# A cross-attention stack, second layer: the output bias as one product of three bf16 parts, reciprocals a quarter ahead, queries ahead at the layer's borders

## The reference, cut to what matters

```python
# L1: 32 query heads of 8, 8 key/value heads
q, k, v = x @ Wq + bq, ctx @ Wk + bk, ctx @ Wv + bv
attn = softmax(q k^T / sqrt(8) + mask)          # over 64 context tokens
out  = (attn v).reshape(b, l, H) @ Wo + bo
x    = layer_norm(out + x) * gamma + beta
```

## Time and profile before

| what | us |
|---|---|
| runs | 1150.19, 1145.28, 1144.76 |
| median | 1145.28 |
| the profiled execution | 1143.87 |
| its span, first to last instruction | 1141.9 |
| PE busy | 1062.1 (93% of the span) |
| DVE, ACT, POOL busy | 626.7, 490.8, 400.0 |
| mean granted clock of TensorE | 0.98 |

### The profile page before, as it was taken

The page is one execution under the profiler, slowest core; times in us unless marked ns, Lnnn a source line. Parts: engine busy times, 40 slices in busy tenths (PEclk is TensorE's granted clock), DMA queues, the critical chain, the costliest instruction groups (busy, mean ns, idle before and its releaser), DMA issues.

```text
span 1141.9 us, 17046 instructions
## 1 busy us (share of the span) xinstructions
PE 1062.1 (93%) x6804; PEld 814.2 (71%) x6804; DVE 626.7 (55%) x1070; ACT 490.8 (43%) x988; POOL 400.0 (35%) x415
## 2 busy tenths in 40 slices
PE   6999899999799799998999999999999999978998
PEld 3666455555567588877777777777777777657997
DVE  3656787787566522761455445675444544564552
ACT  2556676676566322214333233333233333324543
POOL 2534477778866411310221222232122211222230
PEclk9999998998999899999999999999999999999999
DMA  9000000000000350000000013310000000100000
GB/s 309 30 2 1 1 1 1 1 1 1 1 2 1 113 201 1 1 1 1 1 1 1 1 38 111 111 38 1 1 1 1 1 1 6 70 0 1 28 20 28
DMA packets 17043, 32.22 MB, mean 28 GB/s; under 512 B 3522, under 2 KB 8388, under 8 KB 16452
## 3 DMA queue, kind: packets, MB, share of 16 engines
q1 hardware_dynamic: 16964, 31.13, 8.0%
HBM read 29.03 MB, written 2.10 MB: 27 GB/s over the span
## 4 chain that ended last, share of the span: by engine, by line
PE 73%; ACT 11%; POOL 7%; DVE 4%; issue 4%; DMA 0%; POOLq 0%; DVEq 0%; ACTq 0%
PE work L740 10%; PE work L852 10%; PE scores L791 9%; PE work L808 5%; PE scores L704 5%; PE work L717 5%; PE work L841 4%; PE work L542 2%; PE work L418 2%; PE work L591 2%; PE scores L533 2%; PE work L823 2%; PE work L499 2%; POOL pair L1747 2%; PE work L894 1%
## 5 line engine op out<-in xcount | busy, mean ns | idle before, releaser
L852 PE MATMUL work<-pair,probsT 128*128 128x256 f32 x512 | 122.1, 393 | 11.0 <-ACT pair L1626 8.8
L740 PE MATMUL work<-ctxT,w 128*128 128x128 f32 x1024 | 120.2, 275 | 3.5 <-ACT pair L1617 1.6
L1706 POOL TENSOR_SCALAR stat<-stat 128x2 f32<-128x2 f32 (+1 forms) x49 | 11.2, 228 | 320.0 <-DVE stat L961 319.0
L852 PEld LDWEIGHTS work<-pair,probsT 128*128 128x128 f32 x512 | 96.9, 194 | 35.9 <-issue 20.3
L740 PEld LDWEIGHTS work<-ctxT,w 128*128 128x128 f32 x1024 | 118.2, 192 | 5.2 <-issue 3.1
L791 PE MATMUL scores<-pair,act_bufs 128*128 128x512 f32 x256 | 115.2, 592 | 0.0
L1617 ACT ACTIVATE pair<-work 128x512 f32<-128x512 f32 x64 | 38.3, 598 | 154.3 <-PE work L808 154.3
L1607 ACT ACTIVATE kvT<-work,cols 128x128 f32<-128x128 f32 x128 | 36.6, 369 | 154.5 <-PE work L740 154.5
L1847 POOL TENSOR_TENSOR probs<-probs,smax 128x1024 f32<-128x1024 f32 x22 | 42.0, 1909 | 159.2 <-DVE smax L1283 159.2
L1263 DVE TENSOR_REDUCE smax<-scores 128x16 f32<-128x1024 f32 x32 | 39.2, 1225 | 77.1 <-PE scores L791 77.1
L791 PEld LDWEIGHTS scores<-pair,act_bufs 128*128 128x128 f32 x256 | 46.3, 190 | 46.0 <-issue 45.9
(11 more groups left out here) (168 smaller groups left out, 2370.9 us busy)
## 6 DMA issues: line engine op xcount, KB each, us to landing
w<-in_l_wk SPq DMA_DIRECT2D x8, 512.0 KB, 6.2
w<-in_l_wq SPq DMA_DIRECT2D x8, 512.0 KB, 7.6
w<-in_l_wv SPq DMA_DIRECT2D x8, 512.0 KB, 7.4
w<-in_l_wo SPq DMA_DIRECT2D x8, 512.0 KB, 8.1
out<-x SPq DMA_DIRECT2D x8, 256.0 KB, 2.2
x<-in_x SPq DMA_DIRECT2D x1, 1536.0 KB, 9.4
pair<-in_l_fc SPq DMA_DIRECT2D x1, 1024.0 KB, 7.1
pair<-in_l_pr SPq DMA_DIRECT2D x1, 1024.0 KB, 9.1
```

The source lines that it names most:

```text
L740: last = mm(bank[:, h * P:(h + 1) * P], w[:, c, (4 * g + h) * K3:(4 * g + h + 1) * K3], ctxT[:, c, p * P:(p + 1) * P], start=(c == 0), sto ...
L852: last = mm(step_banks(j + 1)[0][:, 0:D], probsT_bufs[j % 2][:, q, :], pv[n % 2][:, bb, q, :], start=(q == 0), stop=(q == GH // 2 - 1))
```

## The change

1. **Bias.** The row `l1_bo` is split once, at the end of DVE's slot 5, into three bf16 rows that sum to it, on partitions 0, 32 and 64 of an otherwise zero tile (`bias_parted`, nine operations on 1x256). In `output` one bf16 product of 96 rows of ones with that tile, repeated for both halves, takes the place of two float32 products of one row.
2. **Reciprocals.** In L1's slots ACT spreads them before the second exponential instead of after `probs_out(tiles[0])`; PE transposes them before the fourth scores instead of after `probs_transposed(tiles[1])`; ACT copies them out before `ln_finish`, `key_diagonal` and the third exponential instead of last; DVE normalises before the fourth maximum instead of after it.
3. **Border slot.** PE projects the queries of unit 17 right behind the source of unit 18, ACT copies them out there, and DVE takes the second tile's maximum before the last late sums. Two waits that guard the bank `work[3]` follow this order.
4. **Queries elsewhere.** In L0 and L2 ACT copies the queries out before `key_diagonal` and the layer norm's `ln_finish` instead of last. PE's order there is unchanged.

```diff
+        bias_parts = nc.alloc_sbuf_tensor_at("bias_parts", [P, D], BF16, offset=at + 4 * CTX)
+        bias_rest = nc.alloc_sbuf_tensor_at("bias_rest", [P, D], F32, offset=at + 4 * CTX + 2 * D)
...
             def output(u):
                 if layer == 1:
-                    e.wait_ge(d_bo, 1)
-                    e.wait_ge(p_const, 5)
+                    e.wait_ge(d_part, 9)
+                    e.wait_ge(p_const, 6)
+                    mm(work[2][:, :], ones_bf[0:96, :], bias_parts[0:96, :].unsqueeze(1).broadcast_to([96, TT, D]),
+                       start=True, stop=False, skip_group_check=True)
                 for t in range(TT):
-                    if layer == 1:
-                        mm(work[2][:, t * D:(t + 1) * D], ones[0:1, :], row("l1_bo")[0:1, :], start=True, stop=False)
...
                     probs_transposed(tiles[0])
                     weighted(u - 1)
+                    reciprocals_transposed(u - 1)
                     scores(*tiles_of(u)[3])
                     probs_transposed(tiles[1])
-                    reciprocals_transposed(u - 1)
...
                     source(u + 2)
+                    queries(u + 1)
                     weighted(u - 1)
...
-                if u + 1 < NU:
+                if u + 1 < NU and len(late) < 2:
                     queries(u + 1)
...
+            def bias_parted():
+                bias, part, rest = row("l1_bo"), bias_parts, bias_rest
+                first, second, third = slice(0, 1), slice(32, 33), slice(64, 65)
+                e.wait_ge(d_bo, 1)
+                e.wait_ge(p_const, 6)
+                for r in (first, second, third):
+                    v.tensor_copy(part[r, :], bias[r, :]).then_inc(d_part, 1)
...
                     tile_sums(tiles[0][0])
+                    unit_normal(u - 1)
                     tile_max(*tiles[3])
-                    unit_normal(u - 1)
...
                     unit_queries(u + 1)
+                    reciprocals_spread(u - 1)
                     exponentials(tiles[1])
                     probs_out(tiles[0])
-                    reciprocals_spread(u - 1)
+                    reciprocals_out(u - 1)
                     if ended[0] == 1:
                         ln_finish(("l1", ended[1]), xb(ended[1]), xb(ended[1]))
                     if UNITS[u + 2][0] == 1:
                         key_diagonal(u + 2)
                     exponentials(tiles[2])
                     probs_out(tiles[1])
-                    reciprocals_out(u - 1)
...
                     probs_out(late[1])
                     unit_source(u + 2)
+                    unit_queries(u + 1)
...
                     exponentials(tiles[1])
+                if u + 1 < NU and len(late) < 2:
+                    unit_queries(u + 1)
                 if u + 2 < NU and UNITS[u + 2][0] == 1:
                     key_diagonal(u + 2)
                 if coming[0] == 2:
...
                     ln_finish(("l2", b), xb(b), norm[b % 3])
-                if u + 1 < NU:
-                    unit_queries(u + 1)
```

More of the change, by code:

```diff
@@ L267, in build @@
         d_sum, d_den, d_lrec, d_lr = (sem(f"d_{n}") for n in ("sum", "den", "lrec", "lr"))
-        d_wl, d_sl, d_hl = (sem(f"d_{n}") for n in ("wl", "sl", "hl"))
+        d_wl, d_sl, d_hl, d_part = (sem(f"d_{n}") for n in ("wl", "sl", "hl", "part"))
         p_const, p_rstd, p_kd, p_half, p_sum, p_spr = (sem(f"p_{n}") for n in ("const", "rstd", "kd", "half", "sum", "spr"))
@@ L492, in queries @@
                 e.wait_ge(a_vd, u + 1)
-                if u < 1 or UNITS[u - 1][0] != 1:
+                if u < 2 or 1 not in (UNITS[u - 1][0], UNITS[u - 2][0]):
                     e.wait_ge(a_rT, u - 1)
@@ L551, in reciprocals_transposed @@
                 e.wait_ge(a_qT, min(u + 2, NU))
-                if u + 1 < NU and UNITS[u + 1][0] == 1:
+                if u + 1 < NU and 1 in (UNITS[u][0], UNITS[u + 1][0]):
                     e.wait_ge(a_qT, u + 3)
@@ L584, in output @@
                 if layer == 1:
-                    e.wait_ge(d_bo, 1)
-                    e.wait_ge(p_const, 5)
+                    e.wait_ge(d_part, 9)
+                    e.wait_ge(p_const, 6)
+                    mm(work[2][:, :], ones_bf[0:96, :], bias_parts[0:96, :].unsqueeze(1).broadcast_to([96, TT, D]),
+                       start=True, stop=False, skip_group_check=True)
                 for t in range(TT):
-                    if layer == 1:
-                        mm(work[2][:, t * D:(t + 1) * D], ones[0:1, :], row("l1_bo")[0:1, :], start=True, stop=False)
                     for c in range(DC):
                         last = mm(work[2][:, t * D:(t + 1) * D], oT_bufs[u % 2][:, c, t * P:(t + 1) * P], w[:, c, :],
-                                  start=(layer != 1 and c == 0), stop=(c == DC - 1))
+                                  start=(layer != 1 and c == 0), stop=(c == DC - 1), skip_group_check=True)
                 last.then_inc(pe_wo, 1)
@@ L1076, in output_bias @@
                 v.tensor_tensor(row(f"l{layer}_bo"), work[2][:, 0:D], row(f"l{layer}_bo"), ALU.add).then_inc(d_bo, 1)
+            def bias_parted():
[5 more added lines that the diff above has]
+                    v.tensor_copy(part[r, :], bias[r, :]).then_inc(d_part, 1)
+                e.wait_ge(d_part, 3)
+                for r in (second, third):
+                    v.tensor_tensor(rest[r, :], bias[r, :], part[r, :], ALU.subtract).then_inc(d_part, 1)
+                e.wait_ge(d_part, 5)
+                for r in (second, third):
+                    v.tensor_copy(part[r, :], rest[r, :]).then_inc(d_part, 1)
+                e.wait_ge(d_part, 7)
+                v.tensor_tensor(rest[third, :], rest[third, :], part[third, :], ALU.subtract).then_inc(d_part, 1)
+                e.wait_ge(d_part, 8)
+                v.tensor_copy(part[third, :], rest[third, :]).then_inc(d_part, 1)
             for a in "12":
@@ L1124, in vector @@
                     output_bias(coming[0])
-                for k in late:
-                    tile_sums(k)
+                if late:
+                    tile_sums(late[0])
+                if len(late) == 2:
+                    tile_max(*tiles[1])
+                    tile_sums(late[1])
                 if 0 < u <= NU:
@@ L1131, in vector @@
                     tile_shifted(*tiles[0])
+                if len(late) == 2:
+                    tile_shifted(*tiles[1])
                 if coming[0] == 2:
@@ L1135, in vector @@
                     ln_stats(("l2", b), xb(b), TT)
-                if tiles:
+                if tiles and len(late) < 2:
                     tile_max(*tiles[1])
@@ L1142, in vector @@
                     tile_sums(tiles[0][0])
+                if u == 5:
+                    bias_parted()
             def mlp_norm(b):
@@ L1778, in gpsimd @@
                 g.memset(mask_row[name][:, :], 0.0).then_inc(p_const, 1)
+            g.memset(bias_parts[:, :], 0.0).then_inc(p_const, 1)
             e.wait_ge(p_const, 5)
```

## The result

| kernel | median us | runs | ratio to before, 95% interval |
|---|---|---|---|
| before (runs of this comparison) | 1147.74 | 1144.76 to 1153.32 | |
| changed | 1135.49 | 1134.14 to 1136.96 | 0.989 [0.984, 0.993] |

The change is faster by 1.1%. Of the profiled executions, the one before took 1143.87 us with a span of 1141.9, the one after 1134.86 with a span of 1133.1: 8.8 us less in the span. Of the 55 executions of the kernel before that stand beside the experiments, some take 1144 to 1147 us at a granted clock of 0.979 to 0.981 and the others 1148 to 1155 us at 0.970 to 0.978, so its medians (1147 to 1150) lie above its profile, which is of the faster kind. So I account for the 8.8, and where a median against the kernel before says more than the profiles do, both are given.

A forecast was written before the change was run, and what follows sets the result against it. The prediction took PE to set the time, with POOL setting the pace in slots 13 to 16. Gains of 2.5, 2.3 and 3.8 us less 1.8 lost made 6.8, from 1145.3 to 1138.5 us; range 1130.5 to 1146.

The forecast's parts named there:

- Bias: Second layer's output: one bf16 product for two float32 ones, 1.05 us less PE work in each of eight slots.
- Reciprocals, slots 8 to 12: ACT's new 1.1 us wait against PE's wait and bias work saved: 0.5 us gained a slot, 2.5 in all.
- Parts: Nine DVE operations at slot 5's end take 1.9 to 3.8 us; cost taken as 0, range 0 to 1.2.
- Slots 13 to 16: Later `ln_finish` delays POOL in slot 13: 1.8 us lost; PE's bias savings in slots 14 to 16 hidden behind POOL.
- Queries: Ends of slots 6 and 7: PE's waits of 1.03 and 1.27 us for the queries' copy go, 2.3 us gained.
- Border: Entry to the third layer: of PE's 5.5 us waiting in five places, 3.8 us gained; ends 0 and 5.5.
- Rest of the program: From about 387 us on: untouched by the change.
- my signs: Profile marks expected after: slots of 18.8 us, no second-layer PE wait on normalisation, low-clock stretches before 390 us within two.
- the free wait: Rival: ACT's new wait before the reciprocals' copy costs nothing, 15.0 us gained in all, 1130.3 us; chance 0.17.
- the small border gain: Rival: POOL's statistics arrive unchanged at the third layer's border, 1 us gained there instead of 3.8, 1141.3 us; chance 0.25.
- The clock rival: Rival: PE's merged 2.6 us wait brings two low-clock windows in each of eight slots, 15 us, 1153.8 us; chance 0.07.

The follow-up runs named there:

- queries_only: The kernel before with only items 3 and 4 of the change (border slot and queries elsewhere): 1138.20 us, ratio 0.992.
- no_border: The changed kernel without item 3, item 4's order then covering the border slot too: 1134.63 us, ratio 0.989.
- split_noborder: `ln_split` without item 3 (the border slot's order): 1124.87 us, ratio 0.980.
- recs_only: The kernel before with only item 2 of the change (the reciprocals' move): 1158.78 us, ratio 1.009.
- recs_ln: `recs_only` with `ln_finish` ahead of the reciprocals' copy on ACT: 1144.08 us, ratio 0.994.
- moved: The changed kernel with the bias parts prepared at the end of DVE's slot 7 instead of slot 5: 1136.08 us, ratio 0.988.
- norecs_moved: `moved` with item 2 (the reciprocals' move) undone on PE, DVE and ACT: 1134.15 us, ratio 0.989.
- ln_split: The changed kernel with `ln_finish` ahead of the reciprocals' copy on ACT and the bias parts' preparation split over slots 5 and 6: 1124.21 us, ratio 0.978.

## Why the prediction was right, and where its terms were off

The direction and the mechanism held: I forecast 1138.5, 6.8 us less; the median is 1135.49, and the profiled span 8.8 us less. Term by term:

- *Bias.* I charged two float32 products against one of bf16 and got 1.05 us. It was 1.33 (3.37 to 2.04): the step "the bias is 1.24 - 0.19" was under-sized by 0.28, because the eight output products now run in one stream of 1.82 us (169.35 to 171.17) where two groups with bias products between took more. In that stream the bf16 product took 0.22 us, start to next start, though it reads 0.38 from start to end. So the small price was right, near the 0.19 of the rows. The Trainium skill, "TensorE: Matmul & The Clock Gate", section "Single matmul latency", gives an estimated 0.38 us for an isolated product of this size; the trace agrees for the time from start to end.
- *Reciprocals, slots 8 to 12.* ACT's new wait, 1.1 predicted, measured 1.13; the late transposes 1.2 later, measured 1.13; PE's wait of 2.6, measured 2.38; the wait before the output, 0.60 predicted to go, gave 0.77. With the bias: 0.5 a slot predicted, 0.96 measured. Five such slots are 4.8 us, and of the rest of the 6.4 us, 1.7 are fewer low-clock windows (clock loss 5.1 and 3.4): before had 132 to 140, 176 to 180 and 196 to 200, after only 184 to 192 and 208 to 212. The step that failed was the size: two small errors of 0.28 and 0.17 added up to as much as the term.
- *Parts.* "I take 0, range 0 to 1.2" was wrong: 1.6 us in slot 6. I took 0.2 to 0.4 us for each operation, and seven of the nine are so; left to themselves all nine would come to an estimated 3.2 us (six casts of 0.28, three subtractions of 0.42, steps of 0.03 between), still over the 2.65. The step that failed is that I priced DVE alone: the two operations that began while POOL ran added 1.4 us, and the nine took 4.6 us, not 3.8 at most. And I put at 0 what I had myself bounded at 1.2.
- *Slots 13 to 16.* POOL waits 1.88 us longer, 1.8 predicted. Up to the second scores of slot 16 nothing shows of it (62.74 and 62.71), but the transposes of that slot's late tile, from the second scores of slot 13, start 67.18 us on instead of 65.15 (279.70 after, 284.29 before): 2.0 us lost, of which undoing item 2 in slot 13 gave back 1.15.
- *Queries.* Slot 7 gave 1.35 (12.40 to 11.05). Slot 6 at 11.06 in every kernel in which the parts did not stand there makes 1.10. Sum 2.45, predicted 2.3.
- *Border.* 4.1 us from the second scores of slot 16 on, against 3.8. With the 2.0 us that stand before the late transposes put where they belong, the border gave 6.1; about 1.7 of these are clock, since windows at 0.57 and 0.61 (288 to 292 and 316 to 320 us) became one of 0.63 (280 to 284). `queries_only`, without the loss of slot 13, takes 72.92 us there against 79.10, with no clock loss against 3.4: apart from clock, an estimated 2.8 us, where I had 3.8. The waits were right to a few tenths, also that the source of unit 19 would be the next bound; but the sum hid which item gives it. The filling of the wait in slot 16 by queries, to which I gave a part, is worth nothing by `no_border` and 0.7 at most by `split_noborder`; item 4's order gives the rest.
- *Rest of the program.* "Untouched" held for its instructions, not for its clock: +1.9 us.

The total came so near in part by luck: 3.9 us more than forecast in slots 8 to 12 and 2.1 more from there to slot 22, against 1.5 less in slots 6 and 7 and 2.5 at the start and behind slot 22, make the 2.0 between 6.8 and 8.8.

Of my signs, the slot is 18.34 where I said 18.8, and PE still waits 0.61 us for the normalisation once, in slot 16. The windows under 0.8 from 20 to 390 us are six instead of seven, within the two that I allowed. Of the rivals, the free wait is excluded by ACT's 1.13 us, the small border gain by the 4.1. The clock rival did not decide the changed kernel, but it decided `recs_only`. The price I gave it, 1.7 us for a window at 0.57, holds for single windows; in `recs_only` a stretch goes on over three windows and costs 5.0. The clock loss up to 380 us is 20.5 there and 8.6 in the changed kernel; which of the other items keeps it small, no run shows. The Trainium skill, "TensorE: Matmul & The Clock Gate", section "Why this matters for your kernels", speaks against long gaps between bursts, and the gap that it names is longer than the 2.38 us here. So my reading of it went further than the page. In the trace of `recs_only` the clock falls to 0.50 behind 2.38 us and in that of `recs_ln` to 0.61 behind 1.40, and the changed kernel, with waits of 2.38 us and more, is faster all the same; the measurements decide.

What stays open: why the clock falls behind five of the six long waits of the changed kernel and not behind the first, and behind some waits of 1.40 us in `recs_ln`, and so how much of any difference of 2 us or less is clock. The profiles of `moved` and `norecs_moved` differ that way by 3.5 us of clock loss between 110 and 300.

## What to carry to other kernels

An engine's idle time in front of an instruction is slack only if it is on no loop: follow the loop once round, from the operation back to itself one slot earlier, before calling it spare. When an instruction that waits for another engine is moved forward in an in-order list, put in front of it everything that is ready; here that one line was worth 7 to 10 us in the medians, about as much as the queries' order (items 3 and 4, 8.3 us in the profile), the best item of the change. A chain of tiny operations is priced by its rows, plus what it meets on other engines at that place, and split over several idle times if it fits none. And an item that loses by itself (item 2) is not a bad item yet: look for what it put behind a wait.

## What the runs showed that I had not expected

- One loop over DVE, POOL and ACT held three of five slots at 19.41 to 19.60 us though PE had less to do, so that taking 1.33 us of PE work a slot away gave 0.91 us a slot there.
- In `recs_only` the same 2.38 us wait as in the changed kernel was followed by 8 us at the lower level of the clock and 4 more at 0.74 and 0.76 in two slots, though PE was busy without a break from 196 us on (4.00 of 4.00 us in three windows).
- On one partition and 256 elements a subtraction took 0.42 us, but 1.39 where it began under a POOL row of 1.49; a cast took 0.28, but 0.71 under a POOL row of 0.79, and in `ln_split` 1.25 (from 101.87) under one of 1.30 (from 101.68). All three end 0.1 to 0.3 us after POOL's. The same operation differs by four times with what POOL does beside it; in all ten kernels with the parts the slow ones lie so, and POOL's row over the slow subtraction is itself 1.47 to 1.49 instead of 1.28 us. That the two engines hold each other up is how I read it; no run took POOL's work away from there.
